# A fused attention and mixture-of-experts kernel: the first ten batches computed in pairs side by side, and the sums of the last stage made by PE

## The reference

```python
def reference(x, ...):                       # x: 16 batches x 256 tokens x 128, float32
    x = layernorm(x + attention(x))          # one head, D = 128, softmax over 256 keys, W_out
    h = x + layer_norm(x, ln1) @ attn_w.T
    t = layer_norm(h, ln2)
    logits = t @ gate_w.T                    # 8 experts
    top_vals, top_idx = top_k(logits, 2)
    comb = softmax(top_vals), scattered to the 8 experts
    for e in range(8):                       # INTER = 512
        out += comb[:, e] * (silu(t @ gate_proj[e].T) * (t @ up_proj[e].T)) @ down_proj[e].T
    return layernorm(x + (h + out))
```

## Time and profile before

| | |
|---|---|
| runs | 402.53, 403.39, 399.04 us; median 402.53 |
| profiled execution | 403.65 us, of it the span of the trace 401.8 us |
| busy share of the span | PE 78%, DVE 68%, ACT 60%, POOL 50% |
| chain that ended last, by engine | PE 61%, DVE 13%, issue 11%, POOL 6%, ACT 5%, DMA 2% |
| mean granted clock of PE | 0.878 of full speed (2.4 GHz); 0.5 is 1.2 GHz |

### The profile page before, as it was taken

One profiled execution on the slowest core, in us unless ns is written; L12 is line 12 of the kernel. 1 busy time (PEld: TensorE's weight loads), 2 busy tenths in 40 slices (PEclk: granted clock), 3 DMA queues, 4 the chain that ended last, 5 costly groups with the idle time before them and its releaser, 6 DMA issues.

```text
span 401.8 us, 8647 instructions
## 1 busy us (share of the span) xinstructions
PE 312.1 (78%) x1972; PEld 267.2 (66%) x1972; DVE 271.3 (68%) x1079; ACT 241.3 (60%) x559; POOL 202.1 (50%) x251
## 2 busy tenths in 40 slices
PE   5645767776899999999999989989999999960000
PEld 4533556564778788888878878778898989850000
DVE  3353465667688688696878887877676766626990
ACT  3243543444668766866777677668777787731551
POOL 0001015565635585475568668588444442336980
PEclk9665575969899999999999999999999999995555
DMA  8234281201231131121112111223211111006851
GB/s 268 87 111 130 81 291 44 62 30 48 67 113 36 41 88 43 34 69 48 42 47 63 49 54 56 56 87 104 62 48 46 41 45 37 14 12 198 233 158 39
DMA packets 31967, 31.96 MB, mean 80 GB/s; under 512 B 4769, under 2 KB 27557, under 8 KB 31920
## 3 DMA queue, kind: packets, MB, share of 16 engines
q1 hardware_dynamic: 23248, 20.78, 18.3%
q0 software_dynamic: 4320, 8.53, 6.5%
q10 hardware_dynamic: 4352, 2.10, 1.7%
HBM read 20.16 MB, written 11.68 MB: 79 GB/s over the span
## 4 chain that ended last, share of the span: by engine, by line
PE 61%; DVE 13%; issue 11%; POOL 6%; ACT 5%; DMA 2%; ACTq 0%; SPq 0%; POOLq 0%; DVEq 0%
PE bank L514 15%; PE bank L467 7%; PE bank L469 7%; PE bank L468 7%; PE bank L500 7%; POOL expert_rows L1115 4%; PE bank L424 4%; PE bank L408 3%; PE bank L386 2%; PE bank L522 2%; PE bank L387 2%; PE bank L415 2%; PE bank L400 2%; DVE xs L1083 2%; DVE hid L1010 1%
## 5 line engine op out<-in xcount | busy, mean ns | idle before, releaser
L1124 POOL DMA_INDIRECT moe_rows<-ysb,xrow x71 | 70.6, 994 | 93.1 <-ACT ysb L661 85.8
L514 PE MATMUL bank<-wd,hidT 128*128 x568 | 76.4, 278 | 4.9 <-ACT t L668 4.1
L514 PEld LDWEIGHTS bank<-wd,hidT 128*128 128x128 f32 x568 | 69.0, 192 | 7.7 <-issue 7.6
L1115 POOL DMA_INDIRECT expert_rows<-rows,place x64 | 62.3, 974 | 22.4 <-issue 16.2
L467 PE MATMUL bank<-w_hi,t_hi 128*128 x142 | 62.6, 441 | 4.4 <-DVE hid L1010 4.3
L469 PE MATMUL bank<-w_hi,t_lo 128*128 x142 | 56.2, 396 | 0.0
L468 PE MATMUL bank<-w_lo,t_hi 128*128 x142 | 55.9, 394 | 0.0
L674 ACT ACTIVATE th<-bank 128x512 f32<-128x512 f32 x71 | 42.5, 599 | 14.3 <-PE bank L469 14.3
L1010 DVE SCALAR_TENSOR_TENSOR hid<-th,bank 128x512 f32<-128x512 f32 x71 | 48.3, 680 | 3.6 <-ACT th L674 3.4
L1014 DVE TENSOR_TENSOR hid<-hid,bank 128x512 f32<-128x512 f32 x71 | 48.8, 687 | 2.4
L687 ACT ACTIVATE hidT<-bank 128x512 f32<-128x512 f32 x71 | 42.5, 599 | 10.8 <-PE bank L500 10.8
(11 more groups left out here) (153 smaller groups left out, 599.6 us busy)
## 6 DMA issues: line engine op xcount, KB each, us to landing
xrow<-expert_rows SPq DMA_DIRECT2D x71, 66.0 KB, 1.9
w_raw<-weights SPq DMA_DIRECT2D x16, 256.0 KB, 2.7
w_raw<-moe_rows SPq DMA_DIRECT2D x16, 256.0 KB, 3.6
xT<-xt SPq DMA_DIRECT2D x8, 256.0 KB, 3.3
wd<-weights SPq DMA_DIRECT2D x4, 512.0 KB, 6.5
out<-xs ACTq DMA_DIRECT2D x16, 128.0 KB, 3.1
xs<-x SPq DMA_DIRECT2D x3, 512.0 KB, 5.0
moe_rows<-ysb,xrow POOLq DMA_INDIRECT x71, 2.3
```

The source lines that it names most:

```text
L514: last = mm(ps_y, hidT[i % 2][:, c * P:(c + 1) * P], wd[:, bass.ds(w + c * P, P)], start=(c == 0), stop=(c == NC - 1))
L1115: G.indirect_dma_start(out=expert_rows[:, :], out_offset=bass.IndirectOffsetOnAxis(ap=place[:, i, k:k + 1], axis=0), in_=rows[:, i, k, :], ...
L1124: G.indirect_dma_start(out=moe_rows[:, :], out_offset=bass.IndirectOffsetOnAxis(ap=xrow[i % XR][:, C_DST:C_DST + 1].bitcast(I32), axis=0), ...
```

## The change

**The fill.** `FILL` = 5: the first five pairs are computed in turns of their own, n = 0 to 4, written out as a loop on each engine. In a turn both batches of pair n go through each step together, the even one in banks 1, 3, 5 and the odd one in banks 0, 2, 4; `qT`, `kT` and `probT` have two buffers. A turn also holds the later steps of the pairs before it: the contexts, residuals and x1 of pair n - 1, `attn_w`, hidden, logits and choice of pair n - 2 (its contexts were made a turn earlier), ranks, places and sends of pair n - 3. Contexts are now in the bank of the values. Steps q begin at `STEADY` = 40, which in a pair's own count is what step 36 was, with the odd batch of pair 4 already further on; `TILE_FROM` is 42, three steps later in a pair's count than 35 was. `second` drops the odd batch's steps for pairs under `FILL`. The weight pieces are dealt over turns 0, 1 and 2 (5, 7, 4). **The tail.** POOL's and DVE's adds are gone. PE sums `xs` and the two loaded rows in PSUM by three products with the identity (`ps_z`), and statistics and output read from there.

```diff
-TILE_FROM = 35
+FILL = 5
+STEADY = CHUNKS * FILL
+TILE_FROM = STEADY + 2
...
-        PIECE_FROM = 1
...
+        PIECES = [(0, 5), (5, 12), (12, 16), (16, 16), (16, 16)]
 
 
         def at(q, r):
-            g, left = divmod(q - r, CHUNKS)
+            g, left = divmod(q - r - CHUNKS // 2, CHUNKS)
             return g if left == 0 and 0 <= g < GROUPS else None
+
...
+        def second(q, r):
+            g = at(q, r)
+            return g if g is not None and g >= FILL else None
...
-        kT = sb("kT", [P, S])
+        qT = ring("qT", [P, S])
+        kT = ring("kT", [P, S])
...
+        probT = ring("probT", [P, NT, S])
...
+        side = lambda b: 1 if b % 2 and b < 2 * FILL else 0
+        in_qp, in_s, in_vo = [banks[1], banks[0]], [banks[3], banks[2]], [banks[5], banks[4]]
...
+        in_a = lambda b: in_nr if b % 2 else banks[6] if b // 2 < FILL - 2 else banks[5]
+        ps_a = lambda b: in_a(b)[:, 0:NT * A_COLS].rearrange("p (t c) -> p t c", t=NT)
...
+        ps_z = lambda b: banks[b % 8][:, 0:NT * D].rearrange("p (t d) -> p t d", t=NT)
...
-                if b >= 1:
-                    pe.wait_ge(sm["pT_sb"], b)
-                mm(ps_q, params[:, WQ:WQ + D], xt_of(b), start=True, stop=True)
-                mm(ps_k, params[:, WK:WK + D], xt_of(b), start=True, stop=True).then_inc(sm["k_ps"], 1)
+                if b >= 2:
+                    pe.wait_ge(sm["pT_sb"], b - 1 if b < 2 * FILL else b)
...
-                if b >= 1:
-                    pe.wait_ge(sm["v_sb"], b)
-                if b % 2 and b >= 3:
-                    pe.wait_ge(sm["zb_done"], b - 2)
...
+                if b >= 2:
+                    pe.wait_ge(sm["y_done"], NT * (b - 1 if b < 2 * FILL else b))
+                if b >= 2 * FILL:
+                    pe.wait_ge(sm["zb_done"], b - 2 if b % 2 else b - 3)
...
-                if b >= 1:
-                    pe.wait_ge(sm["y_done"], NT * b)
+                if b >= 2:
+                    pe.wait_ge(sm["prob_done"], NT * (b - 1 if b < 2 * FILL else b))
...
-                if b % 2 == 0:
-                    pe.wait_ge(sm["v_sb"], min(2 * g + 3, B))
+                if b % 2 == 0 and g >= FILL - 2:
+                    pe.wait_ge(sm["y_done"], NT * min(2 * g + 3, B))
...
-
-            for q in range(6, ALL):
+            for n in range(1, FILL):
+                qk(2 * n)
+                qk(2 * n + 1)
+                if n >= 3:
+                    rank(n - 3)
+                if n >= 2:
+                    turn_n1(n - 2)
+                scores(2 * n)
+                scores(2 * n + 1)
+                if n >= 2:
+                    attn_w(2 * (n - 2))
+                    attn_w(2 * (n - 2) + 1)
+                context(2 * n - 2)
+                context(2 * n - 1)
+                turn_prob(2 * n)
+                turn_prob(2 * n + 1)
+                values(2 * n)
+                values(2 * n + 1)
+            rank(FILL - 3)
+            for q in range(STEADY, ALL):
                 experts(q)
                 front(q)
+
+
+            pe.wait_ge(sm["res_done"], 2 * TOKEN_TILES)
+            pe.wait_ge(sm["ysb_done"], MOE_TILES)
+            for b in range(B):
+                if b >= 8:
+                    pe.wait_ge(sm["o_done"], NT * (b - 7))
+                pe.wait_ge(y_in[b % RING], turn(b))
+                mm(ps_z(b), ident, xs[:, b, :, :], start=True, stop=False)
+                mm(ps_z(b), ident, yin[b % RING][:, :, 0, :], start=False, stop=False)
+                mm(ps_z(b), ident, yin[b % RING][:, :, 1, :], start=False, stop=True).then_inc(sm["z_done"], 1)
 
 
         @block.scalar
...
+
+            def cast(i):
+                act.wait_ge(w_in[i % NWR], turn(i, NWR))
+                A(w_hi[:, :, i * WP:(i + 1) * WP], w_raw[i % NWR][:, :, :], ACT.Copy).then_inc(sm["whi_done"], 1)
+
+            query_key(0)
...
-                late(q)
+            A(wvo[:, :], banks[6][:, 0:D], ACT.Copy).then_inc(sm["wvo_copied"], 1)
+            query_key(1)
+            cast(0)
+            cast(1)
+            softmax(0)
             act.wait_ge(sm["waT_ps"], 1)
             A(wa_T[:, :], banks[6][:, 0:D], ACT.Copy).then_inc(sm["waT_sb"], 1)
-            for q in range(5, ALL):
+            softmax(1)
+            prob_turned(0)
+            values(0)
...
+            for n in range(1, FILL):
+                lo, hi = PIECES[n]
+                third = [lo + (hi - lo) * k // 3 for k in range(4)]
+                query_key(2 * n)
+                query_key(2 * n + 1)
+                if n >= 3:
+                    gap_exp(n - 3)
+                if n >= 2:
+                    n1_turned(n - 2)
+                for i in range(third[0], third[1]):
+                    cast(i)
+                softmax(2 * n)
+                softmax(2 * n + 1)
+                for i in range(third[1], third[2]):
+                    cast(i)
+                prob_turned(2 * n)
+                prob_turned(2 * n + 1)
+                if n >= 2:
+                    second_copy(n - 2)
+                values(2 * n)
+                values(2 * n + 1)
+                for i in range(third[2], third[3]):
+                    cast(i)
+                for j in range(GT if n < FILL - 1 else NT):
+                    x1(n - 1, j)
+            gap_exp(FILL - 3)
+            for q in range(STEADY, ALL):
                 early(q)
                 experts(q)
                 late(q)
...
-                        A(xs[:, b, t, :], xs[:, b, t, :], ACT.Identity,
+                        A(xs[:, b, t, :], ps_z(b)[:, t, :], ACT.Identity,
...
+            for n in range(1, FILL):
+                lo, hi = PIECES[n]
+                third = [lo + (hi - lo) * k // 3 for k in range(4)]
+                if n >= 3:
+                    places(n - 3)
+                for i in range(third[0], third[1]):
+                    split(i)
+                largest(2 * n)
+                largest(2 * n + 1)
+                for i in range(third[1], third[2]):
+                    split(i)
+                if n >= 2:
+                    hidden(2 * (n - 2))
+                    hidden(2 * (n - 2) + 1)
+                    second_variance(n - 2)
+                residual(2 * n - 2)
+                residual(2 * n - 1)
+                variances(n - 1)
+                if n >= 2:
+                    logits(n - 2)
+                    choose(n - 2)
+                for i in range(third[2], third[3]):
+                    split(i)
+                x1_scale(n - 1)
+                if n == FILL - 1:
+                    plan_tiles(1)
+            places(FILL - 3)
+            for q in range(STEADY, ALL):
...
-                    dve.wait_ge(sm["z0_done"], s + 1)
-                    V.tensor_tensor(xs[:, s, :, :], xs[:, s, :, :], yin[s % RING][:, :, 1, :], ALU.add
-                                    ).then_inc(sm["z_done"], 1)
                     dve.wait_ge(sm["z_done"], s + 1)
                     for t in range(NT):
-                        V.bn_stats(st3[:, t, :], xs[:, s, t, :]).then_inc(sm["st3_done"], 1)
+                        V.bn_stats(st3[:, t, :], ps_z(s)[:, t, :]).then_inc(sm["st3_done"], 1)
...
+            for n in range(1, FILL):
+                if n >= 3:
+                    send_rows(n - 3, (0, 1, 2, 3))
+                if n >= 2:
+                    second_root(n - 2)
+                first_root(n - 1)
+                if n >= 3:
+                    send_rows(n - 3, (4, 5, 6, 7))
+            for q in range(STEADY, ALL):
...
-            pool.wait_ge(sm["res_done"], 2 * TOKEN_TILES)
-
             def finish(s, live):
-                if live(0):
-                    pool.wait_ge(y_in[s % RING], turn(s))
-                    G.tensor_tensor(xs[:, s, :, :], xs[:, s, :, :], yin[s % RING][:, :, 0, :], ALU.add
-                                    ).then_inc(sm["z0_done"], 1)
```

243 lines of the change are left out of this document (133 added, 110 removed).

## The result

The changed kernel takes 390.78 us (median of 4 runs, 389.70 to 391.47) against 402.62 for the kernel before beside it: a ratio of 0.972, with a 95% interval of 0.966 to 0.978. The forecast was 392.5 us. The sum was near, but its terms were not: the start came earlier than forecast and the experts' stretch gave back less.

A forecast was written before the change was run, and what follows sets the result against it. The prediction took a chain of waits to bound the fill, PE the experts' stretch and POOL the tail. Parts 2 and 3 gave -8.3 us and the tail -1.5, about -10 from the median 402.53: 392.5 us, range 385 to 399.

The forecast's parts named there:

- Part 1: Fill up to the first tile's load: two batches side by side, first load at 95.7 us against 95.93, nothing won.
- Part 3: Experts' stretch: 3.2 us of PE work moved ahead of it, and 0.7 us gained from looser waits.
- Part 4: Tail: sums on PE, first two 2.6 us each, then 1.4 per batch against 1.72; minus 1.5 us.
- its own sign: Fill: the prediction is wrong if the first load goes out over 4 us from 95.7.
- the bound for 2.4 GHz: Fill: with PE at 2.4 GHz all through, the last send comes at 85.8, minus 7.7 us.
- Rival (2): Fill gets 2.4 GHz nearly throughout: last send at 86 to 88, time 385 to 387 us; 12%.
- The loop: Fill, turns 2 to 4: a once-per-turn chain through all engines sets them, at 19.3, 18.6 and 20.8 us.
- Part 2: First load to first gate product: two nearly empty steps lie between, gate product at 103.3; minus 5.8 us.
- The added 1.4 us: Start of the experts' stretch: first gate and up products take up to 1.4 us more at the lower clock.
- looser waits: Experts' stretch: scores wait for the exponentials, not the residual, so PE idles less; a gain of 0.7 us.
- The cost of bank 5: Experts' stretch: values and wa products now wait for a residual; costed at nothing, plus 5 us at most.
- The slower rival: Tail: PE stays at 1.2 GHz, sixteen sums of 2.6 us, time 409 us; 5%.

The follow-up runs named there:

- scores first: Changed kernel with ACT copying the next pair's q and k ahead of x1 and PE making scores ahead of x1's transposes; 383.03 us, ratio 0.9475.
- Root early: Changed kernel with POOL's second root of pair 3 ahead of the last two sends of pair 2; 387.91 us, ratio 0.9642.
- the kernel with the plan late: Changed kernel, six sends of pair 1 ahead of POOL's roots, DVE's second tile plan behind batch 8's residual; 420.07 us (0.9538), again 391.67 (0.9694).

## Why the prediction was right, point by point

The total came within 1.7 us, and that is partly luck: part 1 was off by 5.5 us one way, parts 3 and 4 by 3.5 us the other. By its own sign (the first load over 4 us from 95.7) the prediction was wrong in part 1.

**Part 1, the fill: the mechanism was right, the size off by 5.5 us.** The forecast had the last send of pair 1 at 92.2 and the load at 95.7, "nothing won"; they came at 86.86 and 90.16. All five turns were 0.6 to 1.7 us shorter than laid out, 6.7 us in sum. The granted clock was 0.80 to 0.91 in turns 2 to 4, where I had taken a place between the two levels; the bound for 2.4 GHz throughout (minus 7.7) was the nearer end. That the clock made the difference is read from the windows alone; no run changes it there. Rival (2), with a last send at 86 to 88, described this part rightly and got only 12%; against it stood that the loop leaves PE idle for half of these turns, and PE was idle for a quarter to two fifths of them. The loop itself held: scores first shows it for the three turns together. They were 17.9 us in the mean, against 19.5 for pairs 3 and 4 one batch at a time, so nearly as long, as written. The list had the copies and scores in the loop at 3.4 us; taking them out gave 2.2 us a turn in the mean.

**Part 2, right.** From the first load to the first gate product: 7.34 us, forecast 7.6 (13.18 before). That is minus 5.8; the forecast's minus 5.8 was minus 5.6 here and the 0.2 us by which its load was earlier. The added 1.4 us for a low clock of the first products was about 0.6 (the second product starts 0.79 us behind the first, the third 0.31, the rest 0.23).

**Part 3, wrong by about 2 us.** PE has 2.6 us less to do in the stretch (239.94 to 237.31), as costed (3.2, less the low clock). But I had looser waits give 0.7 more, and idle time grew by 2.3 us, from 9.9 to 12.2: -0.4 us where -2.5 was forecast. I had searched for the new wait in PE's row (bank 5) and found it covered. The one that cost time was in POOL's and DVE's: the eight sends of pair 2, which stood ahead of the root of pair 3 before as well, now start right behind the late ones of pair 1 and end after the variance is ready, and the logits that wait for the root now stand ahead of the first hidden products. I followed the moved sends only to the first load, not to what stood behind them. Root early recovers 2.25 us of it. The cost of bank 5, taken as 0, was 0 in the changed kernel only by a tie: PE waited 2.83 us for the residual, but the wa product ended at about the time at which the first tile was ready, 92.6. With an earlier load it decides.

**Part 4, right in mean.** Forecast minus 1.5; the kernel before with the new tail gives minus 1.5 by its medians (interval 0.9 to 2.7), the traces minus 1.8 in the mean. The first two sums at 1.2 GHz and then a rise, 1.4 per batch (1.32 with holes), are as written. The rows gave less ground for that rise than the prediction says: it left out the second pair, where PE was busy for 17.58 of 25.49 us at a mean clock of 0.53. The slower rival, PE at 1.2 GHz throughout, did not happen in any of the runs.

**The sum** was -8.3 - 1.5 = -9.8. By the traces it is -5.8 (load), -5.8 (load to gate), -0.4 (stretch), -0.1 (tail) = -12.1; by the medians -11.8. The misses are -5.5 in part 1, -0.2 in part 2, +2.1 in part 3, and +1.4 in this trace's tail, which other executions have less of; they cancel in part.

## What to carry to other kernels

When work is moved on an in-order engine, follow each neighbour that stands behind it, not only the transfer that gates the next stage, and ask when each is ready now: here a root of 1 us stood behind the same eight sends as before, but its variance was ready 3.8 us before POOL came to it, and that took back most of the 2.6 us of PE work that the fill had moved out of the experts' stretch. Where a turn is set by a loop through all engines, look for steps that stand in the row of an engine on the loop and don't belong to it (the copies of q and k ahead of a small exponential); moving them and the scores ahead gave 8 us (383.03 against 390.78), more than any other edit here. And one trace is not enough to call a term of 1 or 2 us nothing: compare several executions of kernels that share the stage, or time the stage alone.

## What the runs showed of the hardware

The clock of the tail rose at different points of the same instruction order: after one sum at the low level in two traces, after nearly two or two in six others, worth up to 1.2 us. Twelve products without use, in time that PE had idle anyway, removed this: in all four traces with them the first sum took 1.37 us and not 2.69. The experts' stretch lasted 247 to 252 us, and PE's busy time for the same products 237.2 to 240.6, with the mean granted clock at 1.00 to 0.98; in four of the nine traces of the new fill on the other chips the clock fell to 1.2 GHz for 6.8 us, beginning 5.9 to 7.4 us behind the first gate product, and PE was busy for 6.0 to 6.7 of them. One chip ran the kernel before in 440.63 us instead of 402.6 to 403.9, with the mean granted clock of those runs at 0.85 to 0.86, where its runs beside the other experiments had 0.88 to 0.89; on it the experts' stretch of the kernel with the plan late was 276.9 us, with PE busy for 249.39 and idle for 27.5 us. Its tail, 40.8 us, was not longer. The cause was not looked into.
